# A decoder layer's first stage: query weights split ahead of the x tiles, first projections interleaved with the transposes of x

## What is computed

```python
x = x + jnp.tanh(g_xattn[0]) * _L0_xattn_ref(_layernorm(x, axis=-1), ctx_4096, Wq, Wk, Wv, Wo, q_norm_w, k_norm_w)
# inside, with latents = layernorm(x):
q = (latents @ Wq).reshape(bsz, q_len, HEADS, HEAD_DIM).transpose(0, 2, 1, 3)
q = rms_norm(q, q_norm_w)
scores = jnp.einsum('bhgqd,bhkd->bhgqk', qg, k) * scale
```

## Time and profile before

| | |
|---|---|
| time, median of 3 runs | 3195.52 us (3192.04 to 3196.73) |
| time of the profiled execution | 3194.47 us |
| its span in the profile | 3191.4 us |
| PE busy | 3006.7 us, 94% of the span |
| DVE, ACT, POOL busy | 2464.5, 2051.1, 1329.4 us |
| DMA over the whole span | 66 GB/s |
| last PE work of `prepare` | transposes at 244.39 us |

### The profile page before, as it was taken

The page is one execution under the profiler, slowest core; times in us unless marked ns, Lnnn a source line. Parts: engine busy times, 40 slices in busy tenths (PEclk is TensorE's granted clock), DMA queues, the critical chain, the costliest instruction groups (busy, mean ns, idle before and its releaser), DMA issues. The chain is left out here.

```text
span 3191.4 us, 51782 instructions
## 1 busy us (share of the span) xinstructions
PE 3006.7 (94%) x14650; PEld 2447.2 (77%) x14650; DVE 2464.5 (77%) x3317; ACT 2051.1 (64%) x2899; POOL 1329.4 (42%) x791
## 2 busy tenths in 40 slices
PE   6995999999899999998999999999999997797899
PEld 5884788888678888886788888778888885585677
DVE  6773888888968888887788888868888888413765
ACT  3443777777857778876787777767787886311211
POOL 1330455555525555554355555535555555000000
PEclk9997999999999999998999999999999998898899
DMA  6973101011211100102111110210010000734200
GB/s 229 276 232 115 37 34 39 33 37 46 75 35 34 45 33 33 35 34 85 34 34 43 36 36 33 73 51 31 33 48 34 33 27 10 228 94 135 91 30 20
DMA packets 183907, 210.87 MB, mean 66 GB/s; under 512 B 10964, under 2 KB 125652, under 8 KB 182760
## 3 DMA queue, kind: packets, MB, share of 16 engines
q1 hardware_dynamic: 179016, 196.27, 19.0%
q0 software_dynamic: 2176, 8.39, 0.8%
q10 hardware_dynamic: 2592, 4.72, 0.5%
HBM read 140.14 MB, written 69.21 MB: 66 GB/s over the span
## 5 line engine op out<-in xcount | busy, mean ns | idle before, releaser
L873 POOL TENSOR_TENSOR att_sm<-att_sm,att_sc 128x1024 f32<-128x1024 f32 (+1 forms) x384 | 854.3, 2225 | 675.1 <-DVE att_pr L824 674.7
L679 PE MATMUL att_ppv<-att_pr,att_V 128*128 128x512 f32 (+1 forms) x2880 | 849.8, 404 | 25.6 <-DVE att_pr L824 22.9
L659 PE MATMUL att_pqk<-att_q,att_kT 128*128 128x512 f32 (+1 forms) x2880 | 850.8, 405 | 6.1 <-issue 3.1
L751 ACT ACTIVATE att_sc<-att_pqk,att_rk 128x512 f32<-128x512 f32 (+1 forms) x960 | 661.1, 689 | 184.4 <-PE att_pqk L659 181.8
L620 PE MATMUL att_pkv<-att_ctxT,att_wkv 128*128 128x512 f32 (+1 forms) x3072 | 762.2, 378 | 1.1 <-DVE att_kT L840 0.5
L824 DVE TENSOR_TENSOR att_pr<-att_sc,att_pr 128x1024 fp32r<-128x1024 f32 (+1 forms) x512 | 643.9, 1258 | 39.2 <-ACT att_pr L762 39.1
L620 PEld LDWEIGHTS att_pkv<-att_ctxT,att_wkv 128*128 128x128 f32 x3072 | 564.8, 191 | 121.7 <-DVE att_kT L840 1.2
L679 PEld LDWEIGHTS att_ppv<-att_pr,att_V 128*128 128x128 f32 (+1 forms) x2880 | 533.4, 191 | 153.4 <-DVE att_pr L824 39.5
L659 PEld LDWEIGHTS att_pqk<-att_q,att_kT 128*128 128x128 f32 (+1 forms) x2880 | 506.1, 185 | 121.8 <-ACT att_sc L751 14.3
L818 DVE TENSOR_TENSOR att_sc<-att_sc,att_pmax 128x1024 f32<-128x1024 f32 (+1 forms) x512 | 585.0, 1143 | 16.9 <-PE att_pmax L628 16.8
L762 ACT CAST att_pr<-att_sc 128x1024 fp32r<-128x1024 f32 (+1 forms) x512 | 510.4, 997 | 113.0 <-PE att_ppv L679 111.5
(11 more groups left out here) (131 smaller groups left out, 2687.4 us busy)
## 6 DMA issues: line engine op xcount, KB each, us to landing
q_scr<-pre_qT SPq DMA_DIRECT2D x128, 256.0 KB, 3.5
att_wkv<-kv_scr SPq DMA_DIRECT2D x64, 512.0 KB, 3.9
att_q<-q_scr SPq DMA_DIRECT2D x64, 512.0 KB, 4.2
o_scr<-att_on SPq DMA_DIRECT2D x64, 256.0 KB, 2.0
out_oraw<-o_scr SPq DMA_DIRECT2D x64, 256.0 KB, 4.7
att_sc<-in_ctx SPq DMA_DIRECT2D x16, 768.0 KB, 4.9
pre_wq_raw<-in_L_xattn_Wq SPq DMA_DIRECT2D x8, 1024.0 KB, 7.2
kv_scr<-pre_kv SPq DMA_DIRECT2D x8, 1024.0 KB, 7.7
```

Source lines behind the costliest of these rows:

```text
L659: mm = pe.matmul(pqk[0:m, (h * NT + t) % 2], kT[:, kp, t * P:t * P + m], q[:, qp, h], start=(i == 0), stop=(i == 2))
L679: mm = pe.matmul(ppv[:], V[0:m, vp, t], pr[0:m, pp, (t // 2) % NP, t % 2], start=(t == 0 and i == 0), stop=(t == NT - 1 and i == 2))
L751: act.activation(sc[0:m, h, t], pqk[0:m, s % 2], ACT.Copy, scale=rk[0:m, t:t + 1]).then_inc(sc_ok, 1)
L873: pool.tensor_tensor(sm[0:m, 0:w], sm[0:m, 0:w], sc[0:m, h, i:i + w], ALU.add).then_inc(sum_ok, w)
```

## The change

The loops over the tiles of x disappear, and their steps get places on the pipeline's axis, in a list `first` that is emitted only once, in the first round. The first head's weight steps keep their places -5.5 to -3, and so now stand in each engine's program ahead of most of the work on x. The resulting orders, up to the first query transpose and a little behind it:

- PE: xt0, xt1, xt2, q0, xt3, xt4, q1, xt5, xt6, q2, xt7, wait for all `xlo` ("xdone"), qt0, q3, qt1, q4, qt2, ...
- ACT: whi, kvhi, xhi0, xhi1, xhi2, xhi3, xhi4, sq0, xhi5, sq1, wait for `wcol`, xhi6, xhi7, whi of the second head, qhi0, sq2, ...
- DVE: xn0, xn1, wlo, kvlo, xlo0, xn2, xlo1, xn3, xlo2, xn4, xlo3, xn5, ss0, xlo4, xn6, xlo5, xn7, qn0, `wcol`, ss1, xlo6, xlo7, qn1, ss2, qlo0, wlo of the second head, qn2, ...
- SP: loads, kvst, lat0, qst0, loads, qst1, kvst, qst2, lat1, qst3, ...

Each of the first 8 projections now waits for its own tile's `xlo`; "lat" stands 1.6 places later. No instruction of computation or transfer is added or removed.

```diff
         steps.sort()
+        first = [(3.1 + 3 * b, "lat", 0, b) for b in range(B)] + [(1.9, "wcol", 0, 0), (2.6, "xdone", 0, 0)]
+        for t in range(QT):
+            first += [(0.5 * t - 1.2, "xt", 0, t), (0.5 * t - 1.1, "xhi", 0, t), (0.5 * t - 0.9, "xlo", 0, t),
+                      (0.5 * t - 1.85 if t >= 2 else 0.1 * t - 5, "xn", 0, t)]
...
-            def run(eng, emit, first=()):
+            def run(eng, emit):
                 pipeline(eng, KVH // NJ, UT, steps, emit, first)
...
-                run(sp, step, [(1.5 + 3 * b, "lat", 0, b) for b in range(B)])
+                run(sp, step)
...
-                for t in range(QT):
-                    act.wait_ge(xt_ps, t + 1)
-                    act.copy(xT[:, HI, :, t * P:(t + 1) * P],
-                             ptr[:, t % 2].rearrange("p (c r) -> p c r", c=KT)).then_inc(xhi_ok, 1)
-
                 def step(n, what, j, t):
                     k, v = NJ * n + j, n * UT + (j * QT + t)
-                    if what == "whi":
+                    if what == "xhi":
+                        act.wait_ge(xt_ps, t + 1)
+                        act.copy(xT[:, HI, :, t * P:(t + 1) * P],
+                                 ptr[:, t % 2].rearrange("p (c r) -> p c r", c=KT)).then_inc(xhi_ok, 1)
+                    elif what == "wcol":
+                        act.wait_ge(w_ok, 2)
+                    elif what == "whi":
...
-                    if what == "q":
+                    if what == "xt":
+                        pe.wait_ge(xn_ok, t + 1)
+                        if t >= 2:
+                            pe.wait_ge(xlo_ok, t - 1)
+                        for c in range(KT):
+                            last = pe.transpose(ptr[:, t % 2, c * P:(c + 1) * P], xn[:, t % 2, c * P:(c + 1) * P], ident[:])
+                        last.then_inc(xt_ps, 1)
+                    elif what == "xdone":
+                        pe.wait_ge(xlo_ok, QT)
+                    elif what == "q":
+                        if isinstance(n, int) and n == 0 and j == 0:
+                            pe.wait_ge(xlo_ok, t + 1)
...
+                    if what == "xn":
                         if t >= 2:
                             dve.wait_ge(xt_ps, t - 1)
                         dve.tensor_scalar(xn[:, t % 2], xin[:, t], mv[:, t, 0:1], rstd[:, t:t + 1],
                                           ALU.subtract, ALU.mult).then_inc(xn_ok, 1)
...
+                    elif what == "xlo":
+                        dve.wait_ge(xhi_ok, t + 1)
```

More of the change, by code:

```diff
@@ L266, in step @@
                         act.activation(qT[:, t % 4, HI], ptr[:, t % 2], ACT.Copy, scale=wcol[:, 3:4]).then_inc(qhi_ok, 1)
-                act.wait_ge(w_ok, 2)
                 run(act, step)
@@ L314, in _, with step @@
                 dve.wait_ge(rstd_ok, 1)
-                for t in range(QT + 1):
-                    if t < QT:
+                def step(n, what, j, t):
+                    k, v, s = NJ * n + j, n * UT + (j * QT + t), t % 2
+                    if what == "xn":
                         if t >= 2:
@@ L320, in _ @@
                                           ALU.subtract, ALU.mult).then_inc(xn_ok, 1)
[L321 to L326, removed]
-                                          ALU.subtract).then_inc(xlo_ok, 1)
[L328 to L336, removed]
+                    elif what == "xlo":
+                        dve.wait_ge(xhi_ok, t + 1)
+                        dve.tensor_tensor(xT[:, LO, :, t * P:(t + 1) * P],
+                                          ptr[:, t % 2].rearrange("p (c r) -> p c r", c=KT),
+                                          xT[:, HI, :, t * P:(t + 1) * P].bitcast(F32),
+                                          ALU.subtract).then_inc(xlo_ok, 1)
+                    elif what == "wcol":
+                        dve.wait_ge(w_in, 32)
+                        dve.tensor_tensor(wcol[:, 2:3], wcol[:, 0:1], wcol[:, 1:2], ALU.mult).then_inc(w_ok, 1)
+                        dve.wait_ge(w_ok, 1)
+                        dve.tensor_scalar(wcol[:, 3:4], wcol[:, 2:3], SCALE, None, ALU.mult).then_inc(w_ok, 1)
+                        dve.wait_ge(w_ok, 2)
+                    elif what == "wlo":
                         dve.wait_ge(wqhi_ok, AHEAD + k + 1)
```

## The result

The changed kernel takes 3187.36 us (median of 13 runs, 3179.53 to 3191.3), the kernel before 3192.04 us in the runs beside it (median of 13, 3185.5 to 3200.06). The ratio is 0.9976 with a 95% interval of 0.9965 to 0.9986: 7.7 us faster, between 4.5 and 11.2. A later measurement of both gave 0.9972 (0.9961 to 0.9983). The forecast was 3190.5 and a gain of 5.1, with "within 0.2%" as the likeliest case. Two things lie in this. The kernel before, from which the forecast was counted, has a median of 3192.04 in 13 runs and not the 3195.52 of three: that alone is 3.5 us.

The account below looks back on a forecast made before the run. TensorE, busy 94%, was taken as the bound. 10.6 won at q0, less transposes 3.2 and stalls 0.4 and 1.4, led to a gain of 5.1: 3194.47 to 3189.4, plus 1.05, rounded to 3190.5; range 3188.3 to 3193, wide 3187 to 3197.

Parts of the forecast that it names:

- within 0.2%: Whole kernel: time differs from the kernel before by no more than 0.2%, about 6.4 us; chance 0.75.
- The shift of the weights: Before q0: ACT splits the first head's weights from 14.6, DVE's low parts end at 20.0, xt2 starts at 21.1.
- 10.6 earlier than 32.50: Start of q0 on TensorE: 21.9 in place of 32.50, a gain of 10.6 us.
- from 21.9 to 27.0: First projection q0: takes 5.1 us at the low clock level, the same as in the kernel before.
- the early clock: Rival: TensorE's clock rises within q0, up to 2.4 us more gain, time 3188 to 3189.5; chance 0.13.
- xn6's chain: DVE's xn6, behind ss0 and xlo4, ends at 32.1; xt6 stalls 0.4 and q1 can't be closed up wholly.
- The steps from q0's end to q3: TensorE from 27.0 to 37.9: transposes of x between projections, stalls of 0.4 and 1.4; q3 5.3 earlier.
- The xdone stall: TensorE ahead of qt0: idles 1.4 us until xlo7 ends at 37.3.
- From q3 to qt2: qt2 waits for qn2 at 44.1, behind the second head's wlo on DVE; qt2 5.1 to 5.2 earlier.
- The transfers: DMA and SP's changed store order: cost put at 0; the rival, all 5.1 absorbed, 3195.5, had chance 0.12.
- The clock rival: q1 to q5 all at the low clock level because of transposes between projections: 3.3 slower, 3197.8; chance 0.10.
- the wide range: Whole kernel time from 3187 to 3197 us, taking in no change and most of the late clock.

Follow-up runs that it names:

- weights ahead only: Changed kernel with all transposes of x put back before q0, the first head's weights still split ahead of the x tiles; ratio 0.9989 to the kernel before.

## Why the prediction was wrong

- **The shift of the weights** was right: weights at 14.51, xt2 at 20.99, q0 at 21.75, each within 0.15 of its figure. The price, x held up by 2.6 us, too. But "10.6 earlier than 32.50" rested on one execution of the kernel before; by three of it and five of the changed kernel q0 is 11.5 earlier.
- **q0 "from 21.9 to 27.0", "I take the same here"**: this step failed. It took one execution's 5.1 as a constant, and that 5.1 is to the square of q0; to the next start the same execution has 4.8. The term measured 3.8 in the profiled execution, and 3.8 to 5.1 in all, 4.6 in the mean. So it explains 1.3 us of the first profile, and 0.5 in the mean; the kernel before has 4.2 to 5.1 itself. What I had as a rival with a chance of 0.13, the early clock, is an ordinary outcome of either kernel. Its price was mis-sized too: I said that xn6's chain would eat most of it, but from q0's end to q3 it takes 9.9 to 10.0 whether q0 takes 2.8 or 5.1, so what q0 wins reaches q3 whole.
- **The steps from q0's end to q3** were put at 10.9 (27.0 to 37.9) and took 9.9 (25.54 to 35.47), and 9.9 to 10.0 in every profile of the changed kernel. This step failed in all executions alike. It priced a group of four transposes by its busy time, 0.6 (and 0.85 for xt3), though from its start to the next matmul it takes 0.35 (42.87 to 43.22 in the earlier trace rows); its tail runs beside what follows. xt3 and xt4 needed 0.8 together, not 1.5 (25.54 to 26.33), and xt5, xt6 and the stall of 0.3 between them 1.1, not 1.6 (29.17 to 30.25). qt0 took 0.4, not 0.6. The projections took 2.8, not 2.6, which gives back 0.4. The xdone stall was 1.4 as said.
- **From q3 to qt2**, put at 6.2, with a stall behind the second head's wlo, took 6.1 (35.47 to 41.59), and the wait of ACT for wcol cost TensorE nothing, though the slack there was 0.65 and not 1.5: xhi6 waited for wcol until 32.46 and ended at 33.05, xt7's copy began at 33.70.
- **The transfers, "I cost this at 0"**: this step failed too, the other way. q3 to the end takes 202.2 in the mean of the changed kernel and 201.2 in the kernel before, 1.1 longer. The argument that DMA's backlog begins with qst0 and shifts with it was right for the query stores, but "the bytes up to the second round of loads are equal" overlooked the order within them: the moved stores of x fall next to that round. Undoing them gave the beat back.
- **In sum** the stage gained 7.1 in the profiled execution and 6.1 to 6.4 in the mean, not 5.1. At q3 the mean gain is 7.5, not 5.3: 0.9 more from q0's start (11.5 and not 10.6), 0.9 from the steps behind q0 and 0.5 from q0 itself, less 0.1 for the kernel before, where q0 to q3 takes 10.6 in the mean and not 10.7. The transfers take 1.1 of it back. That the forecast came as near as it did is in part luck, since these errors have both signs. The gain of 6.1 is 0.19%, at the very bound that I had set between "same" and "faster". The two ratios say 7.7 and 8.9, and 6.1 lies inside both intervals (4.5 to 11.2, and 5.4 to 12.5). Whether the change is worth more than its first stage gives stays open.
- **The clock rival ("rises late", by the Trainium skill, "TensorE: Matmul & The Clock Gate", Part 4)**: did not happen. The row at 26.33 has q1 at the high level in the first profile (2.8 to the next start), and it is so in all others. With the rule itself the trace agrees so far: eight tiles of transposes from 15.41 on left q0 slow, and so they did with only 1.4 of idle time ahead of q0 (weights ahead only: 4.5). It only does not follow from it that transposes in between hold the clock down. The rival's price did not add up either: q1 to q5 at 2.5 each, less the 5.1 won and less the stalls that could hide a part (0.4, 1.4 and 0.4), is 5.2 slower and not 3.3, outside the wide range.

## What to carry to other kernels

Where a stage starts by preparing one operand and then the other, interleaving by tile is what pays: moving one preparation ahead of the other won 1.4 us here, letting the consumer start on the first tile the other 4.7. Price a group that is put between others by the time from its start to the next start, not by its busy time: that was worth 0.9 us here. Price a stretch that runs at TensorE's low level from more than one execution, as a range, since it differs by about 1 us with nothing changed. And when a schedule is edited, look at which large transfers become neighbours in the queue, not at their sum.

## What the runs showed of the hardware

The time that TensorE lost to the low level in its first dense matmuls varied for the same program: the first twelve matmuls of 512 columns took 3.8 to 5.1 us in five profiles of one kernel and 4.2 to 5.1 in three of the other, where they take 2.8 at the high level. Four transposes of 128x128 between two projections took 0.60 us by their own row and 0.35 from start to next start (42.87 to 43.22). Over the whole kernel executions of one program differ by some 12 us (3179.53 to 3191.3 in 13 runs of the changed kernel), most of it in stages that the change does not touch, and mostly with the mean granted clock: the four runs at 0.976 have spans of 3177.7 to 3179.9, the eight at 0.973 or 0.974 3181.1 to 3188.0, and one at 0.925 has 3189.5. Four 1 MB stores moved 1.6 places later, the last of them directly behind 1.5 MB of loads, cost TensorE about 1.1 us, with the same bytes in all. TensorE's idle time could be filled with useless matmuls to raise the clock ahead of time, which shortened the first stage by 2 to 3 us each time it was tried; the whole kernel did not get shorter by it in any of three measurements, and in two of them it came out 6 us or more longer than a like kernel without them.
